# Expert layer on one core: the chosen expert's low second weight and bias row copied in per row, the image part as pairs of 64-column products

## What is computed

```python
h = gelu(einsum('bth,ehf->betf', x, W1) + b1)
y = einsum('betf,efh->beth', h, W2) + b2
w = scores * one_hot(sel, E)
out = einsum('beth,be->bth', y, w)
```

## Time and profile before

| | |
|---|---|
| runs | 1032.10, 1034.21, 1034.34 us; median 1034.21 |
| the profiled execution | 1031.61 us, its span 1029.8 us |
| mean granted TensorE clock | 0.841 |
| PE busy | 703.4 us (68%) |
| DVE busy | 882.5 us (86%) |
| ACT busy | 709.8 us (69%) |
| expert stage | from 858.9 us to the end of the span |

### The profile page before, as it was taken

One profiled execution on the slowest core, in us unless ns is written; L12 is line 12 of the kernel. 1 busy time (PEld: TensorE's weight loads), 2 busy tenths in 40 slices (PEclk: granted clock), 3 DMA queues, 4 the chain that ended last, 5 costly groups with the idle time before them and its releaser, 6 DMA issues. The chain is left out here.

```text
span 1029.8 us, 22671 instructions
## 1 busy us (share of the span) xinstructions
PE 703.4 (68%) x5955; PEld 480.7 (47%) x5956; DVE 882.5 (86%) x2425; ACT 709.8 (69%) x1374; POOL 166.7 (16%) x274
## 2 busy tenths in 40 slices
PE   3873396747888366676667666666545286999997
PEld 3652244425555233343444433333233155889996
DVE  5898997888888799999999999999977874667766
ACT  0255475947888698898998998899955293545553
POOL 5851310017664000000000000000003530000000
PEclk9996598978999688787787888887856597999999
DMA  8000000001111111111111111111013004455452
GB/s 257 3 2 1 0 1 1 0 1 40 37 37 36 36 28 24 24 29 23 23 25 24 25 24 24 25 24 25 13 51 117 18 1 154 143 183 202 170 195 81
DMA packets 84271, 54.71 MB, mean 53 GB/s; under 512 B 53704, under 2 KB 83176, under 8 KB 83976
## 3 DMA queue, kind: packets, MB, share of 16 engines
q1 hardware_dynamic: 83208, 54.11, 17.3%
q0 software_dynamic: 1024, 0.13, 0.2%
HBM read 11.90 MB, written 3.76 MB: 15 GB/s over the span
## 5 line engine op out<-in xcount | busy, mean ns | idle before, releaser
L1357 DVE SCALAR_TENSOR_TENSOR expo<-expo,con,pow 128x153 f32<-128x153 f32 x480 | 146.2, 377 | 1.2 <-ACT expo L1266 1.2
L1140 PE MATMUL at_rem<-word,ident_half 128*128 128x459 f16 x160 | 65.8, 411 | 103.9 <-ACT expo L1266 102.1
L1266 ACT ACTIVATE expo<-at_rem,con 128x459 f32<-128x459 f32 x160 | 95.3, 639 | 14.1 <-PE at_rem L1141 13.2
L952 DVE TENSOR_REDUCE rs_ends<-rs_banks 128x770 f32 (+1 forms) x96 | 89.1, 958 | 12.5 <-PE rs_banks L924 10.0
L873 ACT ACTIVATE rs_banks<-rs_banks 128x770 f32<-128x770 f32 x96 | 74.3, 796 | 22.6 <-PE rs_banks L916 21.7
L1400 DVE CUSTOM_DVE_ANT_0 weight_top<-weight_top,line 128x2448 uint16<-128x2448 uint16 x64 | 86.2, 1346 | 2.1 <-ACT line L1258 2.1
L1222 ACT ACTIVATE word<-at_banks 128x459 uint8<-128x459 f32 x160 | 80.7, 560 | 10.1 <-PE at_banks L779 10.0
L1140 PEld LDWEIGHTS at_rem<-word,ident_half 128*128 128x128 f16 x160 | 15.7, 98 | 153.7 <-ACT expo L1266 148.1
L1258 ACT ACTIVATE line<-weight_top 128x1224 f32<-128x1224 f32 x64 | 74.0, 1158 | 15.1 <-DVE weight_top L1385 14.8
L774 PE MATMUL at_banks<-pick,row_top 128*128 128x459 bf16 x160 | 73.0, 456 | 11.5 <-ACT word L1222 4.7
L1930 ACT ACTIVATE qk<-e_p,b1s 128x153 f32<-128x153 f32 x192 | 58.7, 391 | 30.1 <-PE e_p L1891 28.9
(11 more groups left out here) (392 smaller groups left out, 2083.2 us busy)
## 6 DMA issues: line engine op xcount, KB each, us to landing
qk<-vt SPq DMA_DIRECT2D x64, 384.0 KB, 3.1
rs_kb<-qk SPq DMA_DIRECT2D x128, 28.7 KB, 1.9
kb<-qk SPq DMA_DIRECT2D x128, 28.7 KB, 1.9
patches<-in_patches SPq DMA_DIRECT2D x4, 768.0 KB
vi<-vt SPq DMA_DIRECT2D x32, 96.0 KB, 2.0
out<-vi SPq DMA_DIRECT2D x32, 96.0 KB, 1.7
pj_w<-in_w SPq DMA_DIRECT2D x1, 2304.0 KB, 8.2
qb<-qk SPq DMA_DIRECT2D x128, 6.0 KB, 1.8
```

The source lines that it names most:

```text
L952: v.tensor_reduce(ends[:, :, n, 5 * b:5 * b + 5], banks[:, slot(u, b), :, 0:5 * W].rearrange("p i (t n) -> p i t n", n=W), AX, ALU.max).th ...
L1140: pe.matmul(out, identh[:, :], bank(word, b).bitcast(F16), start=True, stop=False)
L1266: act.activation(bank(ex, b), rem[:, (u + b) % 2, 0:3 * N], ACT.Square, scale=2.0 ** 24, bias=c(5)).then_inc(sq_done, 1)
L1357: ins = v.scalar_tensor_tensor(ex[:, t, :], ex[:, t, :], c(7), pw[:, t, :].bitcast(BF16), ALU.add, ALU.mult, accum_out=tot[:, t:t + 1])
```

## The change

Each row now also gets a copy of its expert's low second weight (288 KB, 128 runs of 2304 bytes) and of its bias row (96 KB), issued by SyncE behind a new wait for `collect(n-4)`, into four slots each. The slot's semaphore counts 64 for a row instead of 32, and TensorE waits for all four copies ahead of `first_product(n)`. The image part becomes six pairs: the high weight's product goes into `p3[0:64]` as before, the low weight's into `p3[64:128]`, so into other columns of the array. VectorE no longer reads the expert's number: it takes the bias from the slot, and adds `p3[64:96]` in one more instruction.

```diff
@@ -1815,6 +1815,10 @@
         sb = lambda n, s, t=F32: k.sb(n, s, t, st)
         g = m["qkflat"][:, 12288:12288 + 4 * FT * N].bitcast(F32).rearrange("p (u f n) -> p u f n", u=2, f=FT)
         gs = sb("e_gs", [P, 2, FT, N + 32 + NT], BF16)
+        bias2 = m["pj_raw"][:, :, :].rearrange("p a b -> p (a b)")[:, 0:SLOTS * C].rearrange("p (u c) -> p u c", u=SLOTS)
+        wl_own = sb("e_w2_low", [P, 2, FT, C], BF16)
+        wl_line = m["line"][:, :, :].rearrange("p a b -> p (a b)")[:, 2 * FT * B:2 * FT * B + FT * C].bitcast(BF16).rearrange("p (u f c) -> p u f c", u=2, f=FT)
+        wl = [wl_own[:, 0, :, :], wl_own[:, 1, :, :], wl_line[:, 0, :, :], wl_line[:, 1, :, :]]
         ws = m["qkflat"][:, 0:SLOTS * 4 * FF].rearrange("p (s i a f) -> p s i a f", s=SLOTS, i=2, a=2)
         rows_out = m["vi"][:, :, :].rearrange("p a b -> p (a b)").bitcast(F32).rearrange("p (t c) -> p t c", c=C)
         share = m["line"][:, :, :].rearrange("p a b -> p (a b)")[:, 0:2 * FT * B].rearrange("p (e f b) -> p e f b", e=2, f=FT)
@@ -1852,6 +1856,10 @@
                         wait_apart(sp, h_acc, (n - SLOTS) * 2 + 2, k.passed)
                     for i, w in enumerate((w1h, w1l)):
                         sp.dma_start(ws[:, u, i, :, :], w[:, :, e, :]).then_inc(w_in[u], 16)
+                    if not (isinstance(n, int) and n < SLOTS):
+                        wait_apart(sp, i_bias, n - SLOTS + 3, k.passed)
+                    sp.dma_start(wl[u], w2l[:, e, :, :]).then_inc(w_in[u], 16)
+                    sp.dma_start(bias2[:, u, :], b2[:, e, :]).then_inc(w_in[u], 16)
 
                 def rows(n, j, grp):
                     wait_apart(sp, y_out, n + 2, k.passed)
@@ -1882,7 +1890,7 @@
 
                     u = kk % 2
                     pe.wait_ge(h_act, n * FT + FT)
-                    pe.wait_ge(w_in[kk], (n - kk) * 8 + 32)
+                    pe.wait_ge(w_in[kk], (n - kk) * 16 + 64)
                     for f in range(FT):
                         o = p1[:, u, f // 3, (f % 3) * N:(f % 3 + 1) * N]
                         fs = slice(f * P, (f + 1) * P)
@@ -1902,9 +1910,9 @@
                         mm = pe.matmul(p2[:, u, 0:C], gs[:, u, f, a], w[:, e, f, :], start=(b == 0), stop=(b == 3 * FT - 1))
 
                     wait_apart(pe, i_bias, n + 1, k.passed)
-                    parts = [(w, f) for f in range(FT) for w in (w2h, w2l)]
-                    for b, (w, f) in enumerate(parts):
-                        mm = pe.matmul(p3[0:64, u, 0:C], gs[:, u, f, BOTH], w[:, e, f, :], start=(b == 0), stop=(b == 2 * FT - 1))
+                    for f in range(FT):
+                        pe.matmul(p3[0:64, u, 0:C], gs[:, u, f, BOTH], w2h[:, e, f, :], start=(f == 0), stop=(f == FT - 1))
+                        mm = pe.matmul(p3[64:128, u, 0:C], gs[:, u, f, BOTH], wl[slot][:, f, :], start=(f == 0), stop=(f == FT - 1))
                     mm.then_inc(y_acc, 1)
 
                 def body(c, kk):
@@ -1965,18 +1973,20 @@
 
                 def collect(n, j, grp):
                     u, r = j % 2, slice(32 * j, 32 * j + 32)
-                    e = v.value_load(sel[0:1, ds(n, 1)], min_val=0, max_val=E - 1)
                     v.wait_ge(y_acc, n + 1)
+                    v.wait_ge(w_in[j], (n - j) * 16 + 64)
                     v.wait_ge(y_out, n + 1)
-                    v.tensor_tensor(yb[:, u, :], p2[:, u, 0:C], b2[:, e, :], ALU.add).then_inc(y_bias, 1)
+                    v.tensor_tensor(yb[:, u, :], p2[:, u, 0:C], bias2[:, j, :], ALU.add).then_inc(y_bias, 1)
 
                     v.wait_ge(i_out, grp + 1)
-                    v.tensor_tensor(yi[r, :], p3[0:32, u, 0:C], b2[0:32, e, :], ALU.add).then_inc(i_half, 1)
+                    v.tensor_tensor(yi[r, :], p3[0:32, u, 0:C], bias2[0:32, j, :], ALU.add).then_inc(i_half, 1)
                     v.wait_ge(y_bias, n + 3)
                     v.wait_ge(sent[j], (n - j) * 4 + 16)
                     v.scalar_tensor_tensor(ot[:, j, :], yb[:, u, :], gw[:, ds(n, 1)], Hres[:, n, :], ALU.mult, ALU.add).then_inc(y_out, 1)
-                    v.wait_ge(i_half, n + 1)
-                    v.tensor_tensor(yi[r, :], p3[32:64, u, 0:C], yi[r, :], ALU.add).then_inc(i_bias, 1)
+                    v.wait_ge(i_half, n * 2 + 1)
+                    v.tensor_tensor(yi[r, :], p3[32:64, u, 0:C], yi[r, :], ALU.add).then_inc(i_half, 1)
+                    v.wait_ge(i_half, n * 2 + 2)
+                    v.tensor_tensor(yi[r, :], p3[64:96, u, 0:C], yi[r, :], ALU.add).then_inc(i_bias, 1)
 
                 def image(grp):
                     v.wait_ge(i_bias, grp * 4 + 6)
```

## The result

| | before | after |
|---|---|---|
| runs, median | 1033.99 us (1032.10 to 1034.34, 4 runs) | 1053.79 us (1053.02 to 1054.56, 4 runs) |
| the profiled execution, its span | 1031.61, 1029.8 | 1053.02, 1051.2 |
| PE, DVE, ACT busy | 703.4, 882.5, 709.8 | 695.1, 894.2, 710.5 |

The changed kernel takes 1.0196 times as long, 95% interval 1.018 to 1.0212. The two profiled spans differ by 21.4 us.

The account below looks back on a forecast made before the run. TensorE bounded the kernel before; SyncE's issuing would after. Row 4 at 875.9, plus 27 x 5.09 + 6 x 2.03, put the last first product at 1029.9, 14.2 later; less 0.1, 1045.7, called 1046 us, range 1030 to 1058.

Parts of the forecast that it names:

- SyncE becomes the bound: Expert loop: SyncE's issuing needs 5.60 us a row with image stores, TensorE 4.2; chance 0.70.
- The price of a row: SyncE's loop row without image stores: 3.76 + 1.09 + 0.16 + 0.30 - 0.22 = 5.09 us, priced from earlier rows.
- SyncE's room: Expert loop before the change: SyncE works 17.1 of 19.25 us in four rows, 2.15 to spare.
- Rows ahead of the loop: First four rows of the expert stage: two more issues each, 1.41 us a row, row 4 starting 5.6 later.
- Image block: Image stores after every fourth row: 2.03 us of SyncE's work, six blocks in the sum.
- The bias landing: Row 31, end of the loop: the bias copy lands 2.0 us after issue, then the last first product starts.
- The new wait costs nothing: SyncE's copies behind collect(n-4): no cost once SyncE sets the pace; at row 4 at most 1 us, once.
- DMA share: Expert loop: 384 KB more a row raises the DMA share from 0.51 to 0.63, leaving room.
- Pairs: TensorE's image part: six overlapping pairs take about 0.6 us instead of 1.11; worth 0.5 only in the last row.
- Issuing was not hidden: Rival, expert loop: issuing is hidden and TensorE stays the bound, faster, some 1020 us; chance 0.07.
- no issue cost as little as the store's 0.36: Rival, SyncE's added issues cost as little as they can: about no change, 1030 to 1036 us; chance 0.13.
- that rival: TensorE, idling for SyncE, falls to its lower clock: 4 us in all, or 24 if longer; 1050 to 1070; chance 0.10.

Follow-up runs that it names:

- the one-copy run: Against the changed kernel, the first weight's two copies (high and low part) became one copy of 512 runs, same bytes: 1049.82 us, ratio 1.0171.

## Why the prediction was right, and where its sizes were off

- **The time: inside the range,** 1053.79 us where 1046 was forecast and 1030 to 1058 allowed; the sum itself was 7.3 us short, as taken apart below.
- **SyncE becomes the bound: right.** No wait of SyncE in the loop, first weight copies 5.0 to 5.2 us apart (5.0 to 5.2 forecast) and 7.4 in the fourth rows (7.1 forecast), TensorE idle until a bias copy lands. Shown by taking away and adding: the stores off SyncE, 26 us less; the copies off SyncE, 24.5 less; one more copy, 13.7 more.
- **The price of a row: the sum right (5.09 forecast, 5.08 on average over 27 rows), the step that gave it wrong.** The step said that each instruction has a price to be taken from a row of before. In the row at 954.57 the two issues are 0.52 + 0.62 = 1.14 (1.09 forecast), the gaps 0.22 + 0.13 + 0.28 against 0.36 before, 0.27 more (0.46 forecast), the store 0.11 more (0 forecast), the register read with what lies around it 0.29 less (0.22 forecast). The prices hang together, through what is still being copied. That the errors cancelled here was luck; where the same step was used for the one-copy run it missed by 16 us.
- **A sign of this stood in the trace of before.** The prediction took SyncE's room from its steps, 2.15 us in four rows, and read its waits as saying the same. They do not: in those four rows SyncE waited for VectorE 0.8, 1.6 and 0.4 us, 2.8 in all. In the row at 944.34 it waited 0.8 us for its store, and the row came out at 4.03 instead of 3.77:

```profile
946.88 0.36 SPq L1858 DMA_DIRECT2D out<-vi  x1
948.37 1.44 SPq L1854 DMA_DIRECT2D qk<-vt  x2
```

From the end of this store to the next copies it is 948.37 - 947.24 = 1.13 us; in the row without a wait it is 940.58 - 939.02 = 1.56. What stood behind the wait went faster for it, so the prices of before were not fixed either.
- **Rows ahead of the loop: too short by 1.5 us.** Four of them took 17.6 (863.44 to 881.01), not 16.1: with nothing but copies in a row, the bias issue was at 0.70 to 1.10.
- **Image block: too short,** 7.38 - 5.02 = 2.36 instead of 2.03, six times 0.33, 2.0 us; the rows' average gives 0.4 of it back.
- **The bias landing: 2.7 instead of 2.0,** and the last row's way from its first copy to its first product 1037.55 - 1032.24 = 5.31 instead of 4.45, 0.9 us. The row it was taken from the earlier trace rows stood in a stage with few copies beside it.
- **The new wait costs nothing: right**; also at row 4, where 1 us was allowed.
- **DMA share 0.63 forecast, 0.65 measured; the data not the price: right as to bandwidth** (277 GB/s with the same copies issued by ScalarE), but the bytes came back in the price of issuing, which the prediction had not seen.
- **Pairs 0.6 us forecast, 0.62 measured; VectorE's register read gone, an addition of 0.36 added: right,** and neither on the path. Of VectorE's 1.05 us of idle time 0.35 came back as a wait for its own split.
- **The rivals.** Issuing was not hidden, and no issue cost as little as the store's 0.36. The clock fell as that rival said, after four of the six image blocks and for one row (after the other two the first product took 2.22 and 2.23 us), without setting the pace: SyncE, which waits for nobody, can't have been held up by it. By the prediction's own rows one slow row in four could cost nothing: 8.46 + 3 x 4.23 = 21.15 us of TensorE stand against 4 x 5.09 + 2.03 = 22.39 of SyncE. The rival's 4 us left out the time of the image block.

The sum against its own execution: 1045.7 forecast, 1053.0 measured, 7.3 more. 3.6 is the later start, 1.5 the rows ahead of the loop, 1.6 the loop (151.2 instead of 149.6 us), 0.9 the last row, and 0.3 less at the end. The step that was mis-sized is the pricing of issues and landings by rows from quieter stretches.

The rule that the time to initiate a DMA is usually small relative to the DMA (the Trainium skill, "DMA: Bandwidth & Descriptors", section "Issuing engines are not separate DMA queues") holds here for a single one, 0.62 against 2.7 us for the bias row, and still misleads: five issues and a register read made a row of 5 us that TensorE would have done in 4.25.

## What to carry to other kernels

When a change adds small DMAs to an engine that issues in order, lay out that engine's row from the timeline before anything else: its steps without waits, not its busy time, tell how much room there is. Spread issues over engines that have idle time; here the same copies issued by ScalarE turned 2% slower into 0.8% faster. And take the prices from a stretch with as many bytes under way as there will be: saving an issue gains nothing while the next one is held up by the copies ahead.

## What the runs showed of the hardware that was not expected

- The same issue of a 96 KB copy took 0.51 us behind a first weight of 128 KB and 1.24 us behind one of 768 KB, with the same number of copies and runs; a store went from 0.37 to 0.66, a register read from 0.31 to 0.55 us.
- The hold-up is shared: with two copies a row moved to ScalarE, SyncE's store took up to 1.28 us, where 0.387 was the most before.
- TensorE's register read, moved into the middle of the first product, put 0.2 to 0.7 us between the starts of two neighbouring matmuls in 13 of 28 rows: the 15 matmuls ahead of it did not cover it there.
- Two executions of the same kernel started the same stage 4.6 us apart, with 1031.61 and 1035.89 us in all.
